# Sixteen weight splits moved from VectorE to GpSimd in a two-FFN, selective-scan layer

## The chip, the cores and the metric

The kernel runs on one core of a Trainium2 chip. The metric is device time in microseconds; lower is better. One core has TensorE (PE in the profile; its weight loads are PEld), VectorE (DVE), ScalarE (ACT), GpSimd (POOL) and SyncE (SP), which here issues the DMAs. Each engine takes its instructions in the order in which they were emitted and waits on semaphores that others raise.

## The reference

Input x is 4 x 1024 x 512 in float32: 4096 rows. The layer is half a feed-forward net, a selective scan, and half a feed-forward net again, each on the normalised rows and each with a residual:

```python
x = x + 0.5 * ffn(layernorm(x))
x = x + attn(layernorm(x))
x = x + 0.5 * ffn(layernorm(x))          # same weights as the first

def ffn(x):                               # gate_w, up_w: 1408 x 512, down_w: 512 x 1408, entries -1, 0, 1
    return ((silu(x @ gate_w.T * gate_s) * (x @ up_w.T * up_s)) @ down_w.T) * down_s

def attn(x):                              # I = 1024 channels, N = 16 states
    h, gate = split(W_in @ x)             # W_in: 2048 x 512
    h = silu(causal_conv4(h) + conv_b)
    ts, B, C = split(Wx @ h)              # 128, 16, 16; each rms-normalised
    delta = softplus(Wdt @ ts + dt_bias)
    # per channel i and state n, over the 1024 time steps of a sequence:
    # s = exp(delta * A[i, n]) * s + delta * B[n] * h ;  y += s * C[n]
    return Wout @ ((y + D * h) * silu(gate))
```

## The kernel before

**Precision.** A matmul in the kernel takes float32 data split in two: a high half that ScalarE makes by copying to TensorE's format, and a low half, the difference between the data and the high half. A product is then the sum of three matmuls (`PARTS`: high by high, high by low, low by high). The weights stand in DRAM as 57 pieces of 128 x 512. All have to be split once. At first use a raw piece is loaded, its high half is written by ScalarE and its low half by the subtraction in question, both into a slot of `wring` (three slots), and the slot is stored to the DRAM buffer `wsp`, from which later uses load it ready-made. The 33 feed-forward pieces are only checked: the reference's weights there are small integers, so that their low halves are zero, and the program takes the branch that leaves them out (`light`). The first three of `W_in`'s pieces and five more are split in the early part from a staging area in `sbuf` (`late` is false: 8 pieces). The other sixteen are the "late" ones, and they alone bear on the change: eight for the gate half of `W_in` (stage `gates`, chunk 0) and eight for `Wout` (stage `post`, chunk 0). Their raw data is loaded into `tb[:, 0..3]` (L1953), ScalarE makes the high half (L1553), VectorE the low half (L1730), and SP stores the slot (L1966).

**Tiling.** The rows are cut in eight chunks (`c`) of 512; two chunks make one sequence. Per chunk there are the stages `ffn1`, `prep_in` (the W_in product, convolution), `dt0` to `dt3` (softplus), `post` (gating and W_out product) and `ffn2`. They form the main stream. Beside it runs the scan stream: per chunk 32 groups (two halves of four 128-channel blocks, 16 states each). For one group GpSimd multiplies delta*h by the row of B (L1890, two instructions of 128 x 1024), ScalarE makes four exponentials (L1517, into two PSUM banks `pa`), VectorE does four scans (L1691), TensorE transposes the result (L1367), and VectorE adds C times it to `acc` (L1702). For three of the sixteen states ScalarE (L1538) and GpSimd (L1903) do this last step. Buffers: `sbuf` three deep, the row of B (`bring`, L2092) two deep. `post` of a chunk comes three chunks behind.

**The rest of GpSimd's work.** It makes the low halves of activations (L1765 in the nets and `post`, L1806 in `prep_in`), residual sums (L1775), and parts of the softplus (L1816 to L1827).

**What sets the order.** `Book` lists the units of every thread (`m` main, `c` convolution, `l` norms, `d` softplus, `s` scan products, exponentials and scans, `t` transposes and sums, `z` setup and weight pieces; the DMAs have one thread each) with the semaphore values that they wait for. `Plan.order` then runs all threads through a model of the engines' durations (`Sketch`) and writes out one fixed order per engine: again and again it takes the unit with the least start time plus 0.01 us times its rank (`FIRST`). On VectorE, `z` has rank 1, before everything but the norms. `FIRST` has no entry for `z` on GpSimd, and a thread without one has rank 9 (`rank.get(name, 9)`), behind the scan's rank 4. Because every choice depends on the model's clock, a changed duration or engine of one unit can change the order of all that follows. In each engine's program a wait holds up everything behind it. In SP's queue the store of a piece (L1966) waits for the low half, and DMAs that stand behind it wait too.

**What waits for a low half.** TensorE's first matmul on the slot (`ring_tok[k] = u.lo`; L1310 in `gates`, L1299 in `post`), the store (L1966), and the next raw load into the same place (`late_tok`).

Of the kernel before, what the change touches and what calls it, by code (L numbers as in the profile page):

```python
# [49 lines left out]
ALU = mybir.AluOpType  # L50
# [203 lines left out]
class Book:  # L254
# [56 lines left out]
    def staged(self, kind, n, slot, k, there, before, late=False):  # L311

        u = self.add("z", Unit(kind))
        u.n, u.slot, u.k, u.there, u.before, u.late = n, slot, k, there, before, late
        u.hi = self.up(self.S.a_piece)
        u.lo = self.up(self.S.v_piece)
        if kind == "checked":
            u.kept = self.pieces[n] = self.up(self.S.st_p[k], 16)
            self.check = u.lo
        else:  # L320
            u.kept = self.pieces[n] = self.up(self.S.st_q[k], 16)
        if not late:
            self.raw_free[k] = (u.lo,)
        self.add("piece_out", u)
        return u
# [778 lines left out]
def macaron(nc, x_in, wp_in, wx_in, wdt_in, const_in, lnw_in, ds_in, ident_in, out):  # L1104
    ctx = ExitStack()
    with ctx:
# [6 lines left out]
        def sem(name):  # L1113
            return ctx.enter_context(nc.semaphore(name))
# [64 lines left out]
        S = Unit("semaphores")  # L1179
# [13 lines left out]
        S.v_g, S.v_tslo, S.v_yu, S.v_yg = sem("v_g"), sem("v_tslo"), sem("v_yu"), sem("v_yg")  # L1193
        S.v_scan, S.v_cmac = sem("v_scan"), sem("v_cmac")

        S.g_const, S.g_one, S.g_ve, S.g_rs, S.g_nb = sem("g_const"), sem("g_one"), sem("g_ve"), sem("g_rs"), sem("g_nb")
        S.g_lo, S.g_sum, S.g_halo, S.g_clo = sem("g_lo"), sem("g_sum"), sem("g_halo"), sem("g_clo")
        S.g_xs, S.g_rr, S.g_bc, S.g_bn, S.g_ct = sem("g_xs"), sem("g_rr"), sem("g_bc"), sem("g_bn"), sem("g_ct")
# [20 lines left out]
        def col(i, n=1):  # L1219
            return cst[:, i:i + n]  # L1220
# [24 lines left out]
        def staged_in(u):  # L1245
            return tb[:, u.k, :] if u.late else sbuf[:, 0, u.k, :]

        def staged_out(u):
            return parts[:, u.slot, :, :].bitcast(F32R) if u.kind == "part" else wring[:, u.slot, :, :]
# [457 lines left out]
        def dve_pieces(units):  # L1707
            def program(q, e):
                for u in units:
                    if u.kind == "consts":  # L1710
                        q.wait_ge(u.there)
                        e.tensor_scalar(csh[:, 0:11], col(C_GS, 11), 0.5, None, ALU.mult).then_inc(S.v_const, 1)
                        yield
                        q.wait_ge(u.gs)
                        e.tensor_tensor(csh[:, 11:22], csh[:, 0:11], col(C_US, 11), ALU.mult)
                        yield
                        e.tensor_scalar(dsb[:, :], dsb[:, :], 0.5, None, ALU.mult)
                        yield
                        e.tensor_scalar(csh[:, 22:66], col(C_DS, 44), 0.5, None, ALU.mult).then_inc(S.v_const, 1)
                        yield  # L1720
                    elif u.kind == "checked":
                        s, half = u.slot
                        q.wait_ge(u.hi)
                        e.scalar_tensor_tensor(staged_in(u), staged_in(u), 1.0, wring[:, s, half, :].bitcast(F32),
                                               ALU.mult, ALU.not_equal,
                                               accum_out=losum[:, u.n:u.n + 1]).then_inc(S.v_piece, 1)
                        yield
                    elif u.kind in ("whole", "part"):
                        q.wait_ge(u.hi)
                        e.tensor_tensor(staged_out(u)[:, 1, :], staged_in(u), staged_out(u)[:, 0, :],  # L1730
                                        ALU.subtract).then_inc(S.v_piece, 1)
                        yield
                    elif u.kind == "flag":
                        q.wait_ge(u.check)
                        e.tensor_reduce(lored[:, 0:1], losum[:, :], mybir.AxisListType.X, ALU.add).then_inc(S.v_flag, 1)
                        yield
                        q.wait_ge(u.sum)
                        e.tensor_scalar(lored[:, 1:2], lored[:, 0:1], 0.0, None, ALU.is_gt).then_inc(S.v_flag, 1)
                        yield
                        q.wait_ge(u.pe)  # L1740
                        e.tensor_copy(flag[:, :], pt[0][0:1, 0:1]).then_inc(S.v_flag, 1)
                        yield
                    elif u.kind == "split_x":
                        q.wait_ge(u.hi)
                        m = slice(u.a * small_m, (u.a + 1) * small_m)
                        e.tensor_tensor(wx_flat[:, 1, m], small_stage[u.a], wx_flat[:, 0, m],
                                        ALU.subtract).then_inc(S.v_small, 1)
                        yield
                    elif u.kind == "split_dt":
                        q.wait_ge(u.there)  # L1750
                        e.tensor_scalar(wd_stage, wd_stage, col(C_TLN), None, ALU.mult).then_inc(S.v_small, 1)
                        yield
                        q.wait_ge(u.hi)
                        e.tensor_tensor(wdts[:, 1, :], wd_stage, wdts[:, 0, :], ALU.subtract).then_inc(S.v_small, 1)
                        yield
            return program
# [150 lines left out]
        def pool_consts(units):  # L1907
            def program(q, e):
                for u in units:
                    if u.kind == "consts":  # L1910
                        e.memset(mone[:, :], -1.0)
                        yield
                        e.memset(mhalf[:, :], -0.5)
                        yield
                        e.memset(bn[:, :, :], 0.0).then_inc(S.g_const, 1)
                        yield
                    elif u.kind == "flag":
                        e.memset(lored[:, 2:3], 1.0).then_inc(S.g_one, 1)
                        yield
            return program  # L1920

# [313 lines left out]
```

## Time and profile before

| | us |
|---|---|
| median of 3 runs | 2909.91 (2907.37 to 2915.78) |
| the profiled execution's own time | 2897.91 |
| its span, first to last instruction | 2896.1 |
| PE / PEld busy | 2419.9 / 1961.3 |
| DVE busy | 2496.7 |
| ACT busy | 1756.8 |
| POOL busy | 2259.9 |

Busy times say how long an engine had an instruction in execution; an instruction that is held up in execution counts as busy. A row of a timeline gives start, duration, engine, line and operation; consecutive instructions of one kind are merged ("x3"), and the bracket gives the idle time before them and what ended it. All times are microseconds from the span's start.

### The profile page before, as it was taken

The numbers are of one execution on the slowest core, as the hardware profiler recorded it, in microseconds if no ns is written. First come the engines' busy times: TensorE is split into PE (matmuls) and PEld (weight loads), VectorE is DVE, ScalarE is ACT, GpSimd is POOL, SyncE is SP. The second block draws the span as 40 slices with busy tenths as digits, with TensorE's granted clock in tenths as the row PEclk, the third lists the DMA queues.
The fourth block names the chain that finished last, engine by engine and source line by source line (L and its number), as shares of the span: only waits on it lengthen the run. The fifth ranks groups of instructions, "written<-read, shape, count | busy, mean of one in ns | idle before, by whom it ended". The sixth has DMA issues, their size and how long they took to land. (4 is left out here: it accounts for less than half of the span.)

```text
span 2896.1 us, 38161 instructions
## 1 busy us (share of the span) xinstructions
PE 2419.9 (84%) x12266; PEld 1961.3 (68%) x12266; DVE 2496.7 (86%) x3131; ACT 1756.8 (61%) x2995; POOL 2259.9 (78%) x1370
## 2 busy tenths in 40 slices
PE   6678879788777998889988899889988896599968
PEld 5466667667665876677766777667766775377757
DVE  5549899799889999899989988798988888999973
ACT  5447568667466665576657665667656667465522
POOL 2237859988976889689997889779896799889852
PEclk9869889899888999899998999889999897599989
DMA  7635573673677467945777366854678378355544
GB/s 269 238 114 167 178 241 107 224 264 121 234 263 260 116 201 254 323 163 186 230 266 285 121 223 226 309 206 149 219 253 289 130 260 307 105 194 189 189 163 142
DMA packets 293951, 606.65 MB, mean 209 GB/s; under 512 B 23024, under 2 KB 23792, under 8 KB 293744
## 3 DMA queue, kind: packets, MB, share of 16 engines
q1 hardware_dynamic: 293744, 604.13, 62.1%
q8 instruction: 101, 1.65, 0.2%
q14 instruction: 106, 0.87, 0.1%
HBM read 451.47 MB, written 152.57 MB: 209 GB/s over the span
## 5 line engine op out<-in xcount | busy, mean ns | idle before, releaser
L1890 POOL TENSOR_TENSOR sbuf<-dus,bring 128x1024 f32<-128x1024 f32 x512 | 1220.9, 2400 | 235.0 <-PE pt L1367 130.3
L1517 ACT ACTIVATE pa<-dls,cst 128x512 f32<-128x512 f32 x1024 | 691.5, 688 | 425.8 <-DVE sbuf L1691 419.2
L1367 PE MATMUL pt<-ident,sbuf 128*128 128x128 f32 x4096 | 660.8, 298 | 230.2 <-DVE sbuf L1691 99.8
L1367 PEld LDWEIGHTS pt<-ident,sbuf 128*128 128x128 f32 x4096 | 513.7, 152 | 392.4 <-DVE sbuf L1691 140.6
L1287 PE MATMUL pm<-xT,wring 128*128 128x512 f32 x2816 | 705.7, 399 | 10.7 <-DVE xT L1574 4.3
L1691 DVE TENSOR_TENSOR_SCAN sbuf<-pa,sbuf 128x512 f32<-128x512 f32 x512 | 608.6, 1211 | 65.6 <-ACT pa L1517 55.7
L1691 DVE TENSOR_TENSOR_SCAN sbuf<-pa,carry,sbuf 128x512 f32<-128x512 f32 x512 | 635.0, 1269 | 25.8 <-ACT pa L1517 19.5
L1702 DVE SCALAR_TENSOR_TENSOR acc<-pt,cT,acc 128x512 f32<-128x512 f32 x768 | 548.5, 739 | 78.4 <-PE pt L1367 74.9
L1299 PE MATMUL pm<-wring,act 128*128 128x512 f32 x2176 | 579.7, 409 | 33.2 <-DMA wring<-wsp 11.2
L1287 PEld LDWEIGHTS pm<-xT,wring 128*128 128x128 f32 x2816 | 516.8, 189 | 113.4 <-issue 14.2
L1310 PE MATMUL pm<-xT,wring 128*128 128x512 f32 x1536 | 427.8, 430 | 74.2 <-DVE hd L1641 29.5
L1299 PEld LDWEIGHTS pm<-wring,act 128*128 128x128 f32 x2176 | 401.4, 193 | 120.7 <-DVE hd L1619 16.0
L1310 PEld LDWEIGHTS pm<-xT,wring 128*128 128x128 f32 x1536 | 308.1, 208 | 148.0 <-issue 56.3
L1765 POOL TENSOR_TENSOR act<-hd,act 128x512 fp32r<-128x512 f32 x240 | 310.2, 1298 | 116.6 <-ACT act L1400 115.7
L1903 POOL TENSOR_TENSOR acc<-acc,tmp 128x512 f32<-128x512 f32 x192 | 248.1, 1292 | 45.5 <-ACT tmp L1538 45.1
L1400 ACT ACTIVATE act<-hd 128x512 fp32r<-128x512 f32 x240 | 149.1, 623 | 89.1 <-DVE hd L1619 71.7
L1538 ACT ACTIVATE tmp<-pt,cT 128x512 f32<-128x512 f32 x192 | 130.9, 682 | 89.2 <-POOL acc L1903 76.4
L1396 ACT ACTIVATE th<-pm,csh 128x512 f32<-128x512 f32 x176 | 119.9, 681 | 84.6 <-PE pm L1287 84.0
L1579 DVE SCALAR_TENSOR_TENSOR aa<-th,pm 128x512 f32<-128x512 f32 x176 | 118.1, 671 | 50.4 <-ACT th L1396 50.0
L1323 PE MATMUL pm<-wxs,act 128*128 128x160 f32 x768 | 131.8, 332 | 19.4 <-DVE hd L1641 19.4
L1583 DVE SCALAR_TENSOR_TENSOR hd<-aa,csh,pm 128x512 f32<-128x512 f32 x176 | 129.8, 738 | 17.1 <-PE pm L1287 12.5
L1806 POOL TENSOR_TENSOR act<-hd,act 128x512 fp32r<-128x512 f32 x64 | 82.1, 1283 | 74.9 <-ACT act L1458 69.8
(129 smaller groups left out, 2286.1 us busy)
## 6 DMA issues: line engine op xcount, KB each, us to landing
wring<-wsp SPq DMA_DIRECT2D x408, 512.0 KB, 4.6
bring<-b_d SPq DMA_DIRECT2D x256, 256.0 KB, 4.0
xn_d<-tb SPq DMA_DIRECT2D x24, 1024.0 KB, 9.6
xnb<-xn_d SPq DMA_DIRECT2D x19, 1024.0 KB, 7.4
x_d<-tb SPq DMA_DIRECT2D x16, 1024.0 KB, 6.0
u_d<-hd SPq DMA_DIRECT2D x64, 256.0 KB, 4.5
sg_d<-hd SPq DMA_DIRECT2D x64, 256.0 KB, 4.0
tb<-x_d SPq DMA_DIRECT2D x16, 1024.0 KB, 7.0
```

What stands on the lines that cost most here:

```text
L1287: ins = e.matmul(pm[b][:, :], wring[:, slot, up if light else pw, k * P:(k + 1) * P], xT[:, px, k, :], start=(pw, px, k) == (0, 0, 0), sto ...
L1299: ins = e.matmul(pm[u.bank[tt]][:, :], act[:, px, u.k, tt * P:(tt + 1) * P], wring[:, u.slot, pw + u.half, :], start=u.first and (pw, px) ...
L1310: ins = e.matmul(pm[u.bank][:, :], wring[:, u.slot, pw, k * P:(k + 1) * P], xT[:, px, k, :], start=(pw, px, k) == (0, 0, 0), stop=end)
L1323: ins = e.matmul(pm[u.bank[tt // 2]][:, (tt % 2) * XW:(tt % 2 + 1) * XW], act[:, pw, u.k, tt * P:(tt + 1) * P], wxs[:, px, u.k, :], start= ...
L1367: ins = e.matmul(pt[u.pt[tt]][:, k * P:(k + 1) * P], sbuf[:, u.s3, k, tt * P:(tt + 1) * P], ident[:, :], is_transpose=True, start=True, st ...
L1400: e.activation(act[:, 0, u.k, :], hd[:, u.h, :], ACT.Copy).then_inc(S.a_hi, 1)
L1517: e.activation(pa[k % 2][:, :], dls[:, k, :], ACT.Exp, scale=col(C_A + (4 * u.ig + k) * N + u.n)).then_inc(S.a_exp, 1)
L1691: e.tensor_tensor_scan(d, pa[k % 2][:, :], d, init, ALU.mult, ALU.add).then_inc(S.v_scan, 1)
L1702: e.scalar_tensor_tensor(acc[:, tt, :], pt[u.pt[tt]][:, :], cT[:, u.c % 4, tt, u.n:u.n + 1], acc[:, tt, :], ALU.mult, ALU.add).then_inc(S. ...
L1765: e.tensor_tensor(act[:, 1, u.k, :], hd[:, u.h, :], act[:, 0, u.k, :], ALU.subtract).then_inc(S.g_lo, 1)
L1890: e.tensor_tensor(sbuf[:, u.s3, h * m:(h + 1) * m, :], dus[:, h * m:(h + 1) * m, :], bring[:, u.s2:u.s2 + 1, :].broadcast_to([P, m, TC]), ...
L1903: e.tensor_tensor(acc[:, tt, :], acc[:, tt, :], tmp[:, :], ALU.add).then_inc(S.g_cadd, 1)
```

## The change

The low half of a late piece is now made by a GpSimd unit in thread `z`, with a semaphore of its own. All who waited for the old one wait for the new one. The operation, its operands and the number of instructions are the same. Units that are not late stay on VectorE. Nothing is added to `FIRST`.

```diff
@@ staged
-        u.lo = self.up(self.S.v_piece)
+        u.lo = self.up(self.S.g_piece if late else self.S.v_piece)
@@ macaron
+        S.g_piece = sem("g_piece")
@@ dve_pieces
-                    elif u.kind in ("whole", "part"):
+                    elif u.kind in ("whole", "part") and not u.late:
                         q.wait_ge(u.hi)
                         e.tensor_tensor(staged_out(u)[:, 1, :], staged_in(u), staged_out(u)[:, 0, :],
                                         ALU.subtract).then_inc(S.v_piece, 1)
@@ pool_consts
+                    elif u.kind == "whole" and u.late:
+                        q.wait_ge(u.hi)
+                        e.tensor_tensor(staged_out(u)[:, 1, :], staged_in(u), staged_out(u)[:, 0, :],
+                                        ALU.subtract).then_inc(S.g_piece, 1)
+                        yield
```

## Rows read from the trace of the kernel before

**Rows 1.** The page's busy times (share of the span) and instruction counts
```profile
PE 2419.9 (84%) x12266; PEld 1961.3 (68%) x12266; DVE 2496.7 (86%) x3131; ACT 1756.8 (61%) x2995; POOL 2259.9 (78%) x1370
```
**Rows 2.** Busy time by stretch: start:end, length, engines, granted clock, DMA share, GB/s
```profile
200.00:2797.00 2597.00, 2209.56 (x11370) 1786.93 (x11371) 2361.10 (x2883) 1641.78 (x2792) 2188.78 (x1292) 0.91 0.63 212
```
**Rows 3.** The same view of L1730 alone: DVE busy and count by stretch
```profile
130.00:180.00 50.00, 2.05 (x3) 0.62 0.49 178
180.00:215.00 35.00, 11.27 (x5) 0.81 0.34 120
755.00:800.00 45.00, 9.10 (x2) 0.81 0.53 186
800.00:835.00 35.00, 10.29 (x6) 0.90 0.80 280
```
**Rows 4.** The timeline of VectorE
```profile
138.11 0.68 DVE L1730 TENSOR_TENSOR wring<-tb,wring 128x512 fp32r<-128x512 f32 x1
...
198.94 8.38 DVE L1730 TENSOR_TENSOR wring<-tb,wring 128x512 fp32r<-128x512 f32 x3
207.25 1.21 DVE L1691 TENSOR_TENSOR_SCAN sbuf<-pa,sbuf 128x512 f32<-128x512 f32 x1
...
210.31 2.19 DVE L1730 TENSOR_TENSOR wring<-tb,wring 128x512 fp32r<-128x512 f32 x1
...
755.41 0.75 DVE L1702 SCALAR_TENSOR_TENSOR acc<-pt,cT,acc 128x512 f32<-128x512 f32 x1 [8.14 <-PE pt L1367]
...
763.31 7.53 DVE L1730 TENSOR_TENSOR wring<-tb,wring 128x512 fp32r<-128x512 f32 x1
...
777.03 1.57 DVE L1730 TENSOR_TENSOR wring<-tb,wring 128x512 fp32r<-128x512 f32 x1
```
**Rows 5.** The timeline of GpSimd
```profile
198.07 3.15 POOL L1890 TENSOR_TENSOR sbuf<-dus,bring 128x1024 f32<-128x1024 f32 x1
...
204.07 7.89 POOL L1890 TENSOR_TENSOR sbuf<-dus,bring 128x1024 f32<-128x1024 f32 x3
220.09 13.96 POOL L1890 TENSOR_TENSOR sbuf<-dus,bring 128x1024 f32<-128x1024 f32 x6 [8.13 <-DMA bring<-b_d]
...
760.89 9.41 POOL L1890 TENSOR_TENSOR sbuf<-dus,bring 128x1024 f32<-128x1024 f32 x4
775.66 5.15 POOL L1890 TENSOR_TENSOR sbuf<-dus,bring 128x1024 f32<-128x1024 f32 x2 [5.36 <-DMA bring<-b_d]
```
**Rows 6.** The timeline of SP's DMA issues
```profile
212.53 0.32 SPq L1966 DMA_DIRECT2D wsp<-wring  x1
...
213.44 0.76 SPq L2092 DMA_DIRECT2D bring<-b_d  x1
...
770.87 0.32 SPq L1966 DMA_DIRECT2D wsp<-wring  x1
771.24 1.26 SPq L2092 DMA_DIRECT2D bring<-b_d  x2
```
**Rows 7.** The timeline of TensorE
```profile
201.82 10.88 PE L1310 MATMUL pm<-xT,wring 128*128 128x512 f32 x36 [7.88 <-DVE wring L1730]
...
812.04 2.50 PE L1299 MATMUL pm<-wring,act 128*128 128x512 f32 x5 [3.00 <-DVE wring L1730]
```
**Rows 8.** The page's groups of GpSimd: count, busy, mean ns of one, idle before
```profile
L1890 POOL TENSOR_TENSOR sbuf<-dus,bring 128x1024 f32<-128x1024 f32 x512 | 1220.9, 2400 | 235.0 <-PE pt L1367 130.3
...
L1765 POOL TENSOR_TENSOR act<-hd,act 128x512 fp32r<-128x512 f32 x240 | 310.2, 1298 | 116.6 <-ACT act L1400 115.7
```
**Rows 9.** Groups of GpSimd between 807 and 835
```profile
L1890 POOL TENSOR_TENSOR sbuf<-dus,bring 128x1024 f32<-128x1024 f32 x5 | 13.7, 2743 | 0.0
```
**Rows 10.** Busy time by stretch, columns as in rows 2
```profile
740.00:760.00 20.00, 17.36 (x85) 12.79 (x84) 11.53 (x13) 9.60 (x15) 20.00 (x12) 1.00 0.94 340
760.00:780.00 20.00, 12.22 (x55) 9.60 (x54) 20.00 (x15) 4.90 (x8) 14.64 (x7) 0.83 0.24 70
...
810.00:835.00 25.00, 20.32 (x93) 16.25 (x94) 24.35 (x23) 13.67 (x20) 25.00 (x12) 0.86 0.80 280
```

## The prediction, made before the changed kernel had run

> **What bounds the kernel now.** I read the page's busy times first: VectorE leads with 86% of the span, TensorE has 84%, GpSimd 78% [rows 1]. An average over the whole span hides the start and the tail, so next I asked for the stretch in which scans run, 200 to 2797 us: VectorE is busy 2361.1 of 2597 us, 90.9%, GpSimd 2188.8, 84.3%, TensorE 2209.6, 85.1% [rows 2]. So VectorE is the nearest to a bound, but no engine is full: VectorE's last 9% are short waits in a loop of exponential, scan, transpose and sum. A microsecond taken from VectorE is worth at most one, and one added to GpSimd costs between nothing and one.
>
> Third, the moved instruction by itself. The sixteen late splits stand in four stretches with 2.05, 11.27, 9.10 and 10.29 us, 32.7 us together [rows 3]. That is much more than their work: with GpSimd idle one takes 0.68 us [rows 4], so sixteen would take 10.9. The other 21.8 us are contention, and the timelines show with whom. The split at 763.31 took 7.53 us, to 770.84 [rows 4]; GpSimd ran four products back to back from 760.89 to 770.30, and VectorE's instruction ended half a microsecond after the last [rows 5]. The three at 198.94 took 8.38 us beside GpSimd's products [rows 4, 5].
>
> The Trainium skill (SBUF — State Buffer, "Who interferes with whom") states that a VectorE instruction with two SBUF inputs and a GpSimd instruction that reads SBUF share one port pair, which is an exclusive lock: whoever is first holds it for its whole instruction. The trace agrees that the split is held up, but the rule's "until the first finishes" would let the split in after at most one product, 2.40 + 0.68 = 3.1 us, and the row has 7.53. By the rule alone the excess of 16 pieces would be at most 16 x 2.4 = 38 us, which bounds it no better than the 21.8 that the rows give.
>
> Fourth, who stands behind such a stall. TensorE waited 7.88 us for the first slot in `gates` and 3.00 in `post` [rows 7]. SP had the store of the slot ahead of the next loads of B's row: the store went at 770.87, the loads at 771.24, right after the split ended, and GpSimd, out of rows, idled 5.36 us until 775.66; the same at 212.53 and 213.44 with 8.13 us idle [rows 5, 6]. The plan books far less for the split than it took, so the store stands too early in SP's order. Granted clock was 1.00 at 740 to 760 and 0.83 in the 20 us of the second stall [rows 10], which slows TensorE's work after it; I give that no term of its own.
>
> **The change part by part.** The sum is made against the profiled execution's 2897.91 us.
>
> Removed from VectorE: 32.7 us [rows 3]. Added to GpSimd: 16 x 1.298 = 20.8 us, by the row of the same operation and shape, which reads SBUF twice and writes the same type [rows 8]. It cannot hold itself up. The number of DMAs, their sizes and the ScalarE copies stay.
>
> (a) Three pieces in `prep_in` (0.68 us each, [rows 3, 4]). The main stream is not near their use: cost and gain 0. If the cover were gone it would be 3 x (1.30 - 0.68) = 1.9 us.
>
> (b) Five pieces in `gates`. The first scan starts at 207.25, behind the three held-up splits [rows 4]; its product was ready at 198.07 + 3.15 = 201.22 [rows 5]. So the scan stream can start 6.0 us sooner. Against it: on GpSimd the pieces have rank 9, the products rank 4, so the planner puts them behind the four products that the two rows of B allow. They then come near 209 us and not at 201.8, and the main stream on TensorE stands some 7 us longer. GpSimd's 8.13 us of idle time [rows 5] holds four of the five (4 x 1.30 = 5.2). One stream gains 6, the other loses as much: between 0 and 6.0, and I take 3.
>
> (c) Two pieces at 763 and 777: VectorE loses 9.10 us to them [rows 3]. It is back to back behind each, so the upper end is 9.1. The lower end comes from GpSimd: it was full from 740 to 760 [rows 10], and just before, VectorE had idled 8.14 us waiting for a sum that GpSimd's part held up [rows 4]; if GpSimd is what paces here, the gain is only its idle 5.36 less the two new instructions, 2.6, so 2.8. Halfway is 6.
>
> (d) Six pieces at 811 to 829: VectorE loses 10.29 us [rows 3]. GpSimd is full for all 25 us from 810 to 835 [rows 10] and gets 6 x 1.30 = 7.8 us more. It gets back what the splits cost it: five products took 2743 ns there and not 2400 [rows 8, 9], 1.7 us, and with the other instructions in that stretch, in proportion to its 25 us (25/13.7), some 3.1. Net +4.7 for GpSimd, -10.3 for VectorE. If the two take turns as the bound, 10.3 - 4.7 = 5.6; the ends are -4.7 (GpSimd alone paces) and 10.3. I take 5.
>
> (e) The new wait. GpSimd's instruction waits for ScalarE's high half, made just before. Behind it in GpSimd's program stand products, and behind those the scans. The planner's `Sketch` books 0.16 + 512/474 = 1.24 us for this instruction on GpSimd, and the row has 1.298 [rows 8]; on VectorE it booked 0.05 + 512/962 = 0.58, and the sixteen took 2.04 on average (32.7 / 16). So the wait should now be planned in the right place, as today's was not. 0, and with each of 13 pieces 0.3 us late, 4.
>
> (f) SP. Stores now stand where the plan expects a GpSimd piece to end; the two jams of rows 6 go. This is contained in (b) and (c).
>
> (g) All orders after 138 us are written anew, since the planner's clock moves. Nothing in the rows says in which direction; I carry +-8 us for it, the size of the largest single waits above (8.38 and 8.14) [rows 4].
>
> Sum: 3 + 6 + 5 = 14 us less. 2897.9 - 14 = 2883.9. The median of the runs shown is 2909.9, 12.0 us above the profiled execution; with the same offset the forecast is 2896 us. My own range for this case: the low ends 0 + 2.8 - 4.7 and the high ends 6.0 + 9.1 + 10.3 give -2 to 25 us of gain, so 2885 to 2912; I give it 2885 to 2905 as its core.
>
> **The rivals.**
>
> *VectorE was the whole bound (chance 0.12).* For it: 90.9% busy, and every held-up split is followed by work at once [rows 2, 4]. Then all 32.7 us come back: 2877. Against it: GpSimd is full in two of the three stretches [rows 10], and at 755 VectorE idled 8.14 us.
>
> *Given back later (0.22).* What the scan stream gains is lost at the next place where it waits for the main stream or for GpSimd: b gives nothing, c gives 2.8, d gives 0, and (e) eats it: 2907 to 2910. For it: VectorE idles 9% of the scanning stretch even now [rows 2], so each stream already waits for the other engines at times. Against it: the stalls come while VectorE or GpSimd is full [rows 10], where there is little slack to swallow a gain.
>
> *GpSimd becomes the bound, because its pieces go last (0.18).* Ten pieces are made while GpSimd is busy (four in b, six in d; [rows 4, 10]). With rank 9 each can come behind one product: 2.40 + 1.30 = 3.7 us, 37.0 us in all, as a delay of TensorE's slot. Today TensorE waits 7.88 + 3.00 = 10.9 us for these [rows 7]. So the main stream loses 26.1 us while VectorE gains 14: +12, 2922. It decides from the point where TensorE's waits for the slot exceed some 25 us. For it: GpSimd is full in 740 to 760 and 810 to 835. Against it: three slots. A piece of `Wout` is used for 12 matmuls (four row blocks, three products), and two others stand between its making and its use, so one product's delay should be hidden. The Trainium skill (GPSIMD Engine Reference, "Engine selection") speaks for this rival: elementwise work belongs on VectorE, GpSimd being about twice slower; the rows agree on the ratio, 1.298 to 0.68 us, but leave the stall out of it.
>
> *The change does not do what it says:* all sixteen late units are of the kind "whole", so none is lost between the two new conditions; 0.
>
> **How the numbers follow.** The forecast's case has 0.48, VectorE whole 0.12, given back 0.22, GpSimd bound 0.18. A difference under about 0.3%, 8.7 us, cannot be told from none, so faster is below 2901.2 and slower above 2918.6. Faster: 0.42 of the first, 0.12, 0.02 of the third, together 0.56. Slower: 0.13 of the last, 0.01 of the third, 0.14. The same: 0.30. The range for 8 in 10: 2876, the whole bound, to 2920, short of the last rival's full price.
>
> **What would show it.** L1730 should be left with 8 instructions, and a GpSimd line should have 16 of `wring<-tb,wring` near 1.3 us (right if 1.25 to 1.4; wrong if they too are held up to 3 us). GpSimd's busy time should rise by 16 to 21 us, and VectorE's fall by 30 to 33. The first scan should start near 201 us (b). SP should have no load of B's row behind a late store for more than 2 us, and the two idles of 8.13 and 5.36 us should shrink. TensorE's waits for `wring` from GpSimd should stay under 15 us in total; over 25 the slower rival has it. If VectorE's busy time falls by 30 and the span by less than 5, the gain was given back, and the place is where the two traces' scans, counted from the start, come level again. I am wrong if VectorE's stalls were already covered by GpSimd's pace.

## The result, and the profile after

The changed kernel takes 2936.86 us (median of 4 runs, 2929.07 to 2941.40) against 2908.64 for the kernel before in the same rounds: ratio 1.0089, 95% interval 1.0064 to 1.0115. It is slower. The forecast was 2896 (2876 to 2920), faster; the time is outside the range and on the other side. The profiled execution took 2929.07 us. Ratios here and below leave out the few executions that ran far slower than the rest, two of the twelve of `g_rank35` (3163 and 10567 us) among them.

The page of the changed kernel, span and busy times:

```profile
span 2927.2 us, 38155 instructions
...
PE 2437.4 (83%) x12266; PEld 1977.5 (68%) x12266; DVE 2472.9 (84%) x3115; ACT 1756.2 (60%) x2995; POOL 2278.2 (78%) x1386
```

Beside [rows 1]: VectorE lost 16 instructions and 23.8 us, GpSimd gained 16 and 18.3 us, and yet the span grew by 31.1 us. The move was made and its sizes were nearly those forecast. Of the busy times, the splits' own instructions make up 33.0 and 21.5 us; the rest lies with the other instructions and was not followed. So the time went into waiting. The timeline of GpSimd in `post` of chunk 0 shows where (L1923 is the split, L1891 the product, L1904 the sum, L1817 to L1828 softplus):

```profile
778.98 2.48 POOL L1923 TENSOR_TENSOR wring<-tb,wring 128x512 fp32r<-128x512 f32 x2
...
810.00 2.38 POOL L1891 TENSOR_TENSOR sbuf<-dus,bring 128x1024 f32<-128x1024 f32 x1
812.31 2.38 POOL L1817 TENSOR_TENSOR spw<-spw,spe 128x1024 f32<-128x1024 f32 x1
814.62 4.70 POOL L1891 TENSOR_TENSOR sbuf<-dus,bring 128x1024 f32<-128x1024 f32 x2
...
842.60 2.39 POOL L1891 TENSOR_TENSOR sbuf<-dus,bring 128x1024 f32<-128x1024 f32 x1
844.92 2.55 POOL L1923 TENSOR_TENSOR wring<-tb,wring 128x512 fp32r<-128x512 f32 x2
```

ScalarE's high half of that split:

```profile
812.84 0.63 ACT L1554 ACTIVATE wring<-tb 128x512 fp32r<-128x512 f32 x1 [0.36 <-DMA tb<-wp_in]
```

The high half was ready at 813.47 (812.84 + 0.63) and the split was taken up at 844.92, 31.4 us later. GpSimd had no idle time in between: 16 products, sums and softplus steps, the first of them begun at 812.31, ran before it. TensorE's main matmuls of `Wout` (L1300) by stretch (columns as in rows 2, with PE and PEld alone), then the whole core over the gap:

```profile
740.00:820.00 80.00, 31.81 (x112) 21.48 (x112) 0.86 0.67 234
820.00:845.00 25.00, 0.00 (x0) 0.00 (x0) 0.50 0.38 130
```

```profile
810.00:845.00 35.00, 16.83 (x73) 12.25 (x72) 30.47 (x32) 21.52 (x31) 35.00 (x19) 0.57 0.48 160
```

The main stream stood from 810.45 to 846.27, and TensorE's granted clock fell to 0.50 of full speed, its lower level of 1.2 GHz, while it made only transposes. The view of waits does not show this as one long wait for the slot (TensorE waited for it 5.2 us at most): the planner had put transposes of the scans into the gap. A planned gap shows in no list of waits. It shows when the same instruction is timed in both traces.

The same had happened before, in `gates`. Three of its splits, ready at 198.2, 198.7 and 208.5, were taken up 25.0, 30.4 and 21.8 us later, behind eight products and more:

```profile
223.13 1.27 POOL L1923 TENSOR_TENSOR wring<-tb,wring 128x512 fp32r<-128x512 f32 x1
...
229.03 2.52 POOL L1923 TENSOR_TENSOR wring<-tb,wring 128x512 fp32r<-128x512 f32 x2
```

There the main stream made it good: it was 11 us late at 343 and 1 us at 569. How long a split is held does not say by itself what it costs (`g_gates_only` below tests it).

Lateness against the kernel before of the n-th instruction of a kind (us, positive is later), from the two traces (one execution of each kernel, 31.1 us apart in span where the medians are 28.2 apart):

| at (before) | 241 | 569 | 676 | 845 | 1020 | 1182 | 1348 | 1687 | 2019 | 2297 |
|---|---|---|---|---|---|---|---|---|---|---|
| main stream (low half of xT) | +4.7 | +1.1 | +5.6 | +39.1 | +36.4 | +31.5 | +38.0 | +29.9 | +27.7 | +31.1 |

| at (before) | 245 | 380 | 694 | 834 | 933 | 1218 | 1287 | 1399 | 1575 | 2034 | 2695 |
|---|---|---|---|---|---|---|---|---|---|---|---|
| scans | -7.5 | -22.0 | +0.6 | -14.0 | -40.0 | -56.2 | +14.7 | +21.5 | +27.4 | +27.7 | +31.5 |

The scans ran ahead on what the main stream lost, by 56 us at 1218. Then they met their input. Their products need `dus`, which comes out of the main stream's softplus by way of DRAM. In the changed kernel at the start of chunk 3's scans, from the timelines of VectorE and SP (L2074 stores it, L2090 loads it):

```profile
1164.06 1.27 DVE L1692 TENSOR_TENSOR_SCAN sbuf<-pa,carry,sbuf 128x512 f32<-128x512 f32 x1
...
1203.00 0.43 SPq L2074 DMA_DIRECT2D du_d<-spw  x1
...
1209.85 0.91 SPq L2090 DMA_DIRECT2D dus<-du_d  x2
...
1218.94 2.46 DVE L1692 TENSOR_TENSOR_SCAN sbuf<-pa,carry,sbuf 128x512 f32<-128x512 f32 x2 [3.61 <-POOL sbuf L1891]
```

No scan ran from 1165.33 to 1218.94, and the scans went from 55.5 us ahead to 1.8 ahead in one step. (The list of waits shows little of this too. It puts 3.61 us down to the products, and VectorE's longest idle time in there, 20.01 us before 1207.42, to TensorE's L1300.) The second half of chunk 3 brought the rest, from 9 us late to 27:

```profile
1392.62 9.41 POOL L1891 TENSOR_TENSOR sbuf<-dus,bring 128x1024 f32<-128x1024 f32 x4 [5.98 <-DMA dus<-du_d]
```

From 1575 on both streams are some 24 to 32 us late, to the end.

### The profile page after: what moved, and what is told of

Same layout as the page of the kernel before. It is cut to its first block and busy times, and to the rows that moved or that the text cites. A ratio compares the mean times of both kernels' runs of the same rounds, so it can differ in the third digit from the quotient of the medians.

```text
span 2927.2 us, 38155 instructions
## 1 busy us (share of the span) xinstructions
PE 2437.4 (83%) x12266; PEld 1977.5 (68%) x12266; DVE 2472.9 (84%) x3115; ACT 1756.2 (60%) x2995; POOL 2278.2 (78%) x1386
## 5 line engine op out<-in xcount | busy, mean ns | idle before, releaser
L1891 POOL TENSOR_TENSOR sbuf<-dus,bring 128x1024 f32<-128x1024 f32 x512 | 1216.0, 2391 | 210.4 <-PE pt L1368 96.7
L1368 PE MATMUL pt<-ident,sbuf 128*128 128x128 f32 x4096 | 667.9, 301 | 254.5 <-DVE sbuf L1692 119.5
L1368 PEld LDWEIGHTS pt<-ident,sbuf 128*128 128x128 f32 x4096 | 523.6, 154 | 414.3 <-DVE sbuf L1692 165.0
L1300 PE MATMUL pm<-wring,act 128*128 128x512 f32 x2176 | 578.3, 409 | 30.6 <-DMA wring<-wsp 11.3
L1300 PEld LDWEIGHTS pm<-wring,act 128*128 128x128 f32 x2176 | 401.4, 192 | 119.1 <-DMA wring<-wsp 15.9
L1766 POOL TENSOR_TENSOR act<-hd,act 128x512 fp32r<-128x512 f32 x240 | 311.7, 1303 | 130.0 <-ACT act L1401 129.0
L1904 POOL TENSOR_TENSOR acc<-acc,tmp 128x512 f32<-128x512 f32 x192 | 248.4, 1294 | 57.7 <-ACT tmp L1539 57.7
L1324 PEld LDWEIGHTS pm<-wxs,act 128*128 128x128 f32 x768 | 120.6, 243 | 13.7 <-issue 7.0
```

The costliest lines, as they stand in the source:

```text
L1300: ins = e.matmul(pm[u.bank[tt]][:, :], act[:, px, u.k, tt * P:(tt + 1) * P], wring[:, u.slot, pw + u.half, :], start=u.first and (pw, px) ...
L1324: ins = e.matmul(pm[u.bank[tt // 2]][:, (tt % 2) * XW:(tt % 2 + 1) * XW], act[:, pw, u.k, tt * P:(tt + 1) * P], wxs[:, px, u.k, :], start= ...
L1368: ins = e.matmul(pt[u.pt[tt]][:, k * P:(k + 1) * P], sbuf[:, u.s3, k, tt * P:(tt + 1) * P], ident[:, :], is_transpose=True, start=True, st ...
L1766: e.tensor_tensor(act[:, 1, u.k, :], hd[:, u.h, :], act[:, 0, u.k, :], ALU.subtract).then_inc(S.g_lo, 1)
L1891: e.tensor_tensor(sbuf[:, u.s3, h * m:(h + 1) * m, :], dus[:, h * m:(h + 1) * m, :], bring[:, u.s2:u.s2 + 1, :].broadcast_to([P, m, TC]), ...
L1904: e.tensor_tensor(acc[:, tt, :], acc[:, tt, :], tmp[:, :], ALU.add).then_inc(S.g_cadd, 1)
```

## The experiments

Each is timed against the kernel before in the same rounds. "On GpSimd" and "rank" are those of the late splits.

| label | kernel | median us | ratio (95%) |
|---|---|---|---|
| changed | GpSimd, rank 9 | 2936.86 | 1.0089 (1.0064-1.0115) |
| g_rank1 | GpSimd, rank 1 | 2921.73 | 1.0032 (1.0018-1.0046) |
| g_rank35 | GpSimd, rank 3.5 | 2899.85 | 0.9952 (0.9934-0.9970) |
| g_post_only | eight of `post` on GpSimd, rank 9 | 2953.99 | 1.0133 (1.0104-1.0163) |
| g_gates_only | eight of `gates` on GpSimd, rank 9 | 2909.33 | 0.9988 (0.9970-1.0005) |
| v_rank9 | VectorE, rank 9 | 2965.32 | 1.0185 (1.0156-1.0213) |
| v_margin | VectorE, MARGIN 0.32 | 2930.56 | 1.0073 (1.0047-1.0099) |
| v_margin2 | VectorE, MARGIN 0.27 | 2920.94 | 1.0034 (1.0017-1.0051) |
| g9_m32 | GpSimd, rank 9, MARGIN 0.32 | 2947.68 | 1.0118 (1.0089-1.0148) |
| g9_m27 | GpSimd, rank 9, MARGIN 0.27 | 2947.42 | 1.0128 (1.0101-1.0154) |
| g35_m32 | GpSimd, rank 3.5, MARGIN 0.32 | 2912.16 | 1.0006 (0.9991-1.0021) |
| g35_m27 | GpSimd, rank 3.5, MARGIN 0.27 | 2899.03 | 0.9959 (0.9944-0.9975) |
| v_narrow | VectorE, 8 columns, order of before | 2903.85 | 0.9982 (0.9968-0.9996) |
| v_memset | VectorE, zeros, order of before | 2890.51 | 0.9917 (0.9891-0.9943) |
| g_in_place | GpSimd, order of before | 2904.44 | 0.9980 (0.9963-0.9997) |
| g_held | the same, third split 10 us later | 2909.93 | 0.9991 (0.9973-1.0009) |
| v_early | `Wout` split before `dt0`, VectorE | 2912.80 | 1.0009 (0.9990-1.0027) |

**g_rank1**

```diff
-    "pool": dict(l=0, m=1, c=1, d=2, t=3, s=4),
+    "pool": dict(l=0, z=1, m=1, c=1, d=2, t=3, s=4),
```

> All sixteen late splits on GpSimd as in the changed kernel, but thread z has rank 1 there (it had none, so 9). Theory (starvation by rank): in the changed kernel three pieces of post 0 had their high halves at 813 to 815 us and GpSimd took the first up at 844.92, after 31 us of products, sums and softplus; TensorE's main stream stood from 810.5 to 846.3. With rank 1 that gap must go (TensorE's waits for wring from GpSimd under 5 us), the main stream at post 0 must be no later than in the kernel before, and the time comes to 2885 to 2905 us, that is 30 to 50 below the changed kernel. Rival (GpSimd is simply too slow or too full for them: 20.8 us more work): the time stays within 8 us of the changed kernel's 2937. Rival (any new order of the planner costs some 1%): it also stays well above 2909.

The gap went: the main stream was 23 us ahead of the kernel before at 845 where it had been 39 late. But the time only came down to 2922, 15 of the 28 us, against the 2885 to 2905 expected. Now the scans were late, by 43 us at 834, and the end was paced by them: the main stream was still 7 us ahead at 2297, the scans 42 late at 2417, and both 23 late from 2581. One new wait of VectorE stands right behind splits of `Wout` (GpSimd made three at 794.53 and one each at 802.20, 805.79 and 809.74, with softplus steps between, and only then the sum):

```profile
DVE acc L1703 <- POOL acc L1904: 7.5, 1, 7.5
```

So splits in front of everything on a full GpSimd hold back work for which VectorE waits. That is only part of it. The scans were 28 us late at 712 already, before the first split of `Wout` (756.31), and the version with rank 3.5 below was 25 late there; rank 1 added 15 us by 834, rank 3.5 added 6. What made the first 25 to 28 us was not tried. Nor does this run exclude that an order other than the old one costs its 9 us, whatever the rank; the three margins below bear on that.

**g_post_only, g_gates_only**

```diff
-        u.lo = self.up(self.S.g_piece if late else self.S.v_piece)
+        u.lo = self.up(self.S.g_piece if late and n >= WO else self.S.v_piece)    # gates_only: n < WO
...                                 # the same condition where VectorE and GpSimd emit the split
```

> Only the eight pieces of Wout (stage post) go to GpSimd, rank 9; the eight of gates stay on VectorE. If the gap in post 0 is the cause, this has the same gap of about 30 us in TensorE's main stream and costs 20 to 35 us over the kernel before. If the loss came from the start of the scans (gates), it is within 9 us of before.

> Only the eight pieces of gates go to GpSimd, rank 9; the eight of Wout stay on VectorE. In the changed kernel the main stream was 5 to 12 us late after gates but level again at 568 us, so the theory expects within 9 us of before, 2900 to 2918; the rival (gates, or a new order as such, is the cause) expects over 2925.

Both as the theory had it for the place: the move in `gates` costs nothing, the move in `post` costs it all and more (1.0133, 42 us by the medians, over the 20 to 35 expected). Why it loses more than the changed kernel, 42 us against 28, is open. Its third split began at 852.15, and L1300 paused from 819.8 to 853.46. In `g_gates_only` the splits of `gates` were held just as in the changed kernel (24.9, 30.3 and 21.8 us), and the time did not suffer.

**v_rank9**

```diff
-    "dve": dict(l=0, z=1, m=1, c=1, d=2, t=3, s=4),
+    "dve": dict(l=0, m=1, c=1, d=2, t=3, s=4),
```

> The kernel before with all splits on VectorE, but thread z without a rank there too (9 in place of 1). Theory (the rank starves the pieces on a full engine, whichever it is): the splits in post 0 now come behind VectorE's scans and sums, the main stream stands there, and the time is 10 to 35 us over before. It also holds back the first splits (checked pieces), in which VectorE competes with nothing of a better rank than 1 but the norms and the net's own products, at most 5 us. Rival (rank does not matter, the engine does): within 9 us of before.

The worst of all, 1.0185, above the expected range, with no split on GpSimd. VectorE took up the first two splits of `Wout` 17.2 and 40.8 us after their high halves were ready (0.0 and 0.3 in the kernel before), L1299 paused from 777.14 to 836.84, and the main stream was 49 us late at 845. A rank behind everything starves a split on either of the two engines.

**v_margin, v_margin2: what a new order alone is worth**. `MARGIN` is the time in us that the planner adds, for most threads, before it counts another engine's result as ready. To change it changes the order and nothing else.

```diff
-MARGIN = 0.3
+MARGIN = 0.32        # v_margin2: 0.27
```

> The kernel before with the planner's MARGIN at 0.32 in place of 0.30: the same instructions on the same engines in another order. It measures what a new order alone is worth. Theory (the loss of the changed kernel is the starved splits, not the new order): within 10 us of before. Rival (any new order costs): 15 us or more over before, as the kernel before would then be a lucky order.

> The same with MARGIN at 0.27, a second sample: within 10 us of before by the theory, over 15 above by the rival. Together they give the size of a difference that needs no other cause.

1.0073 and 1.0034, 19 and 9.5 us by the medians: the first lies outside what the theory allowed and inside the rival's range, the second just inside what the theory allowed. The kernel before has a favourable order, and another can start 0.3 to 0.7% behind, though not every one does (`g_gates_only`, 0.9988). So the runs so far leave open how much of the changed kernel's 0.9% is its order. Hence the next four.

Both traces have one wait that the kernel before does not have. Near 2375 VectorE waited 21.6 and 22.9 us for the products, while GpSimd waited 19.2 and 19.4 us for the load of `dus`. The same wait, 20.9 to 22.3 us, stands in `g_post_only`, `v_rank9`, `v_early`, `g35_m32` and both kernels with rank 9 of the next group, and not in the changed kernel or `g_rank35`. The main stream was already 17 and 12 us late at 2297 in the two, so the wait shows where the scans met it and not what delayed it; that stays open.

**g9_m32, g35_m32, g9_m27, g35_m27**: the changed kernel, and the one with `z=3.5` on GpSimd (below), at the two other margins.

> The changed kernel (rank 9) with the planner's MARGIN at 0.32, where the kernel before came to 1.0073. Theory (starved splits cost, whatever the rest): the trace shows splits of Wout held over 15 us behind other GpSimd work, the main stream 20 us or more late by 850 us, and the time is 2930 to 2960. Rival (a bad draw): it is under 2925, or as slow without any gap.

> Rank 3.5 with MARGIN 0.32: 2900 to 2930 by the theory, at least 10 us under the same margin with rank 9. If rank 3.5 at 0.30 was luck, this is as slow as rank 9.

> The changed kernel (rank 9) with MARGIN at 0.27, where the kernel before came to 1.0034: by the theory 2925 to 2955, with the same gap in TensorE's main stream at post 0; by the rival under 2925.

> Rank 3.5 with MARGIN 0.27: 2895 to 2925 by the theory, at least 10 us under rank 9 at the same margin. It also says whether the gain of rank 3.5 over the kernel before (0.9952) holds over a second and third order or was one draw.

Ratios to the kernel before at three margins:

| MARGIN | VectorE, rank 1 | GpSimd, rank 9 | GpSimd, rank 3.5 |
|---|---|---|---|
| 0.27 | 1.0034 | 1.0128 | 0.9959 |
| 0.30 | 1 | 1.0089 | 0.9952 |
| 0.32 | 1.0073 | 1.0118 | 1.0006 |

All four came out in their expected ranges. Along each line the order is the same: rank 9 is 0.5 to 0.9% over VectorE, rank 3.5 is 0.5 to 0.8% under it. Three lines that agree make a mere draw of the order unlikely. The sizes are rough, since another margin changes the rest of the order too and each column differs by 0.4 to 0.7% within itself. About half of the gap is made good later: at equal margin the main stream with rank 9 is 39 to 47 us behind that of VectorE at 845, and 17 to 28 us are left in the medians. The gap is there in all with rank 9; GpSimd's split that was held, at MARGIN 0.32 and 0.27, and TensorE's first main matmul behind it at 0.32:

```profile
844.96 2.53 POOL L1923 TENSOR_TENSOR wring<-tb,wring 128x512 fp32r<-128x512 f32 x2
```

```profile
843.73 2.50 POOL L1923 TENSOR_TENSOR wring<-tb,wring 128x512 fp32r<-128x512 f32 x2
```

```profile
846.30 1.98 PE L1300 MATMUL pm<-wring,act 128*128 128x512 f32 x4
```

The main stream was 38.7 and 40.0 us late at 845.

**g_rank35**

```diff
-    "pool": dict(l=0, m=1, c=1, d=2, t=3, s=4),
+    "pool": dict(l=0, m=1, c=1, d=2, t=3, s=4, z=3.5),
```

> The changed kernel with rank 3.5 for thread z on GpSimd: ahead of the products alone, behind sums, softplus and activations. Rank 9 starved the main stream (+36 us at post 0), rank 1 kept it 22 us ahead but left the scans 43 us behind at 834 us. If a balance is to be found between, it is here: 2900 to 2920, scans and main stream both within 15 us of before at 850 us. If any order that differs costs 10 to 20 us, as the two orders with another margin did (1.0073 and 1.0034), it is 2918 to 2935.

0.9952, at the lower edge of the first range: faster than both kernels, by 11.3 us under the kernel before and 37 under the changed one. Its splits of `Wout` were taken up 0.1 to 3.6 us after their high halves were ready, and the main stream was 26 us ahead at 845. The scans were still 31 us late at 834, not within 15 as expected, but caught up by 2034 (+0.3). This is the version to keep, though at margin 0.32 it is no faster than the kernel before (1.0006). Its page:

```profile
span 2893.6 us, 38162 instructions
...
PE 2423.6 (84%) x12266; PEld 1968.5 (68%) x12266; DVE 2468.1 (85%) x3115; ACT 1757.4 (61%) x2995; POOL 2277.7 (79%) x1386
```

**v_narrow and v_memset: the stall by itself, in the exact order of the kernel before**

```diff
+                        w = 8 if u.late and not isinstance(e, Sketch) else 512
+                        e.tensor_tensor(staged_out(u)[:, 1, 0:w], staged_in(u)[:, 0:w], staged_out(u)[:, 0, 0:w],
...
                         # v_memset, for late units, in place of this:
+                            e.memset(staged_out(u)[:, 1, :].bitcast(F32), 0.0).then_inc(S.v_piece, 1)
```

> The kernel before, in its exact order on every engine, but each late split is emitted 8 columns wide and not 512; the low halves of the gate and Wout weights are left incomplete. It takes most of the 32.7 us of the sixteen from VectorE, adds nothing to GpSimd and moves nothing. Theory (VectorE's held-up splits were covered: where GpSimd is full, VectorE's freed time turns into waiting): the time falls by less than 12 us, VectorE's idle time rises by over 15. Rival (they were on the path, as the forecast had it): it falls by 20 to 33 us. If a narrow split is still held until GpSimd's next gap, its 7.5 us stays, and the trace shows it.

> The kernel before in its exact order, but each late low half is filled with zeros by VectorE (a memset, which reads nothing) and not computed; the gate and Wout products lose that part. In the narrow run a split of 8 columns was still held for up to 7.0 us, so most of the stall stayed; a write without SBUF inputs should not be held (0.2 to 0.7 us each), and VectorE is rid of about 25 to 30 us. Theory (covered: other engines pace there): the time falls by 3 to 15 us, less than half of what VectorE is rid of. Rival (the forecast: VectorE's stalls are on the path): 20 us or more.

VectorE's row for the split of [rows 4] that took 7.53 us, in the narrow run and as a memset:

```profile
763.54 7.00 DVE L1731 TENSOR_TENSOR wring<-tb,wring 128x8 fp32r<-128x8 f32 x1
```

```profile
764.64 0.48 DVE L1731 MEMSET wring<- 128x512 f32 x1
```

With a sixty-fourth of the columns (the other 504 of each low half are left unwritten) it was still held 7 us, so that run freed VectorE of 11.8 us only (2496.7 to 2484.9) and gained 0.18%. The time fell by less than 12 us, as the theory had it, but VectorE's idle time rose by 8.6 us and not by the 15 that it also asked for; this run alone decides little.

The memset reads nothing, is never held (all sixteen 485 ns), frees 22.8 us, and gained 0.83%, 17 to 32 us (20.7 by the medians). That is the rival's value, not the theory's: what held VectorE was on the path in good part. It was not VectorE's time alone. The first split's store went at 765.15 and not at 770.87 (770.57 in the narrow run), so it no longer held up the loads of B's row behind it. GpSimd, which idles 5.36 us before 775.66 in the kernel before ([rows 5]) and 4.86 there in the narrow run, ran six products without a pause from 762.12. There are two reserves. The trace does not show the gain: the run was 10.4 us ahead at 845, behind its last edit, and 5 us late at the end; but that execution (2905.30) was the slowest of the six, the others taking 2883.90 to 2893.48. And the run leaves zeros as the low halves that all later chunks multiply by. How much of the 24 us comes from that data was not tried.

**g_in_place and g_held: the move alone**

```diff
+        moved = [w for w in when["dve"] if w[1] is not None]          # (planned time, piece)
+        out["dve"] = [n for n, w in zip(out["dve"], when["dve"]) if w[1] is None]
+        names, times = out["pool"], [w[0] for w in when["pool"]]
+        for at, piece in moved:
+            at += 0.0                    # g_held: 10.0 for the third piece of Wout
+            i = max(last, next((i for i, t in enumerate(times) if t >= at), len(times)))
+            names.insert(i, "z")
...                                # and GpSimd emits the split where the planner had VectorE
```

> All sixteen late splits on GpSimd, but the planner plans them on VectorE: every other instruction of every engine keeps the order of the kernel before, and each split stands in GpSimd's program at the planned time that it had on VectorE. This is the move alone, without starvation and without a new order. Theory: within 9 us of before, rather under it (2900 to 2915), since VectorE loses stalls that were mostly covered and GpSimd gains 20.8 us where it is full; the loss of the changed kernel is all in the order that the planner made of it. Rival (GpSimd's extra work is the price): 15 us or more over before.

> The same as the kernel in place, but the third split of Wout (and so those behind it) stands 10 us later in GpSimd's program; nothing else differs (31 us as in the changed kernel would make the engines wait for each other in a circle in this order). Theory (a held slot stops TensorE's main stream, and what it loses comes back at the end nearly in full): 6 to 12 us over the kernel in place. Rival (such a delay is swallowed by the two other slots or by slack later): within 3 us of it.

In place the move is worth 0.2%, some 6 us: less than the memset's 24 or so. The rest is what GpSimd's added work can have cost, which is an argument by difference and carries the memset's reserve with it. Held back by 10 us, TensorE's wait for the slot was

```profile
826.39 2.50 PE L1313 MATMUL pm<-wring,act 128*128 128x512 f32 x5 [15.40 <-POOL wring L1938]
```

where it was 5.9 in place, but the time rose by 3 to 5.5 us (ratios, medians), below the expected 6 to 12. The two profiled executions differ by 15, nothing of it made good, but that of `g_held` was the slowest of its twelve. I count this one as inconclusive on the share that is given back.

**v_early**

```diff
+            if c == 0 and self.light:
+                self.split_all(list(range(WO, WO + 8)))
             self.dt0(c)
...                                # and `post` of chunk 0 loads them ready-made
```

> All splits on VectorE, but the eight pieces of Wout are split before dt0 of chunk 0, from sbuf to sbuf and stored to wsp, where VectorE once idled 24 us and GpSimd 20; post 0 then loads them ready-made. No split stands beside a full GpSimd in post 0. If the held-up splits in post 0 (19.4 us of VectorE) were on the path: 8 to 20 us under before. If they were covered: within 8 us of before, 2904 to 2920. A cost of up to 4 us can come at the start, when the raw loads and stores meet the last pieces of W_in.

1.0009. No split stood in `post`, the main stream was 16 us ahead at 845, and the end was 17 us late in the trace. It has a new order too, and two such orders cost 10 and 19 us. The run cannot tell a gain taken back by the order from no gain, so I draw nothing from it.

## Why the prediction was wrong

**The step that failed is (e), the new wait**, and with it the size of the last rival. I wrote that "the wait should now be planned in the right place" and priced it at 0 to 4 us; the rival let each split come "behind one product: 2.40 + 1.30 = 3.7 us". I knew the rank of 9 and took it for a lost tie, once: against the products' 4 it is a handicap of 0.05 us of the planner's clock. In (b) I even let the rank put pieces behind four products, and then priced (e) without it. But on an engine that is full every choice is a tie: each instruction that becomes ready meanwhile has the same earliest start and a better rank. [Rows 10] had shown GpSimd busy 25.00 of 25 us in just this stretch. The split waited for 16 instructions, 31.4 us, and TensorE's main stream stood for 35.8 us. That the rank did it is shown on both engines: with it on VectorE the same stream stops (`v_rank9`), and with 3.5 in its place on GpSimd the holds in `post` shrink to 3.6 us at most, and the time is 1.1 to 1.7% lower at each of three margins. A plan with right durations places such a wait exactly, and exactly too late.

Point by point:

- *Removed and added work.* VectorE 32.7 us less, GpSimd 20.8 more: measured 23.8 and 18.3 as busy time, outside the 30 to 33 and inside the 16 to 21 that I had named. The splits alone come to 33.0 and 21.5, as forecast; the rest is in other instructions. The splits on GpSimd took 1283 ns at the median (1298 forecast), one of them 2247.
- *(a)* Nothing at `prep_in`: g_gates_only, 0.9988, fits.
- *(b)* 3 us from the earlier first scan. It began at 207.1 and not at 201, since the first products (204.62) came after one split and both softplus steps; but the scans were 7.5 us ahead at 245. The later pieces did not come near 209, behind four products, but at 223.13 to 230.3, behind eight and more. `g_gates_only` puts the whole between 9 us gained and 1 lost. The 3 us lie in that interval, as nothing does; the mechanism was wrong.
- *(c), (d)* 11 us from `post`. With the starvation taken away the move is worth 0.5 to 0.8% at equal margin, 14 to 22 us, and rank 3.5 at margin 0.30 gives 2900 where the forecast was 2896. That nearness proves no term of the sum: in the old order (`g_in_place`) the whole move is worth 6 to 7 us of the 14, and no run measures (c) or (d) alone.
- *(f)* The jams of SP went from these two places: GpSimd's waits for B's row were 34.4 us in the kernel before and 25.1 in the changed one. Its waits for `dus` rose from 26.4 to 42.0 instead.
- *(g)* A new order at no cost, +-8 us. Two samples of it cost 10 and 19 us. It should have been a term with a sign: an order that is replaced is rarely replaced by an equal one when the old one is good.
- *The rival "GpSimd becomes the bound"* was the right one in kind, since its pieces did go last, with the wrong price, +12 for +28, and a condition that did not hold as I wrote it ("from the point where TensorE's waits for the slot exceed some 25 us"). Its counter-argument, the three slots, failed because three splits in a row were held: all three slots of the ring stood empty of low halves at once. TensorE's matmuls waited 8.3 us for such a slot in `gates` and 5.2 in `post`, 13.5 together, under the 15 that should have cleared the forecast, since the gap of 35.8 us was planned full of transposes. I had looked for the loss in a list that cannot show it.
- *The rule of the Trainium skill on the lock* (SBUF — State Buffer, "Who interferes with whom"): the narrow run shows that the holding time does not depend on the split's own size (7.00 us with 8 columns, 7.53 with 512), and the memset that an instruction without SBUF inputs is not held (485 ns), as the page says. Nine splits of the narrow run were held over 0.5 us. Eight of them ended within 0.05 us of the end of the GpSimd instruction that ran when they began, which is the rule to the letter. The ninth, the one of 7.00 us, let two such ends pass, at 765.90 and 768.22, and ended 0.02 us after the third, behind which GpSimd had run out of work. No run explains that one.

## What to carry to other kernels

When an operation moves to another engine under a list scheduler, look up its priority there first: on a full engine the lowest rank is not a lost tie but a wait until the engine runs empty, or until what outranks it is done (here 31.4 us), and the stream behind it can stop for as long. What that costs depends on the place: equal holds in `gates` cost nothing. Try at least two or three planner settings on both sides before you credit or blame the move, as two new orders alone cost 0.3 and 0.7% here. And compare the n-th instruction of each stream between traces: a gap that the plan has filled with other work is in no list of waits.

## What the runs showed of the hardware that was not expected

A VectorE subtraction with both inputs in SBUF beside back-to-back GpSimd products was mostly held only until the running GpSimd instruction ended. But at times it was held until GpSimd ran out of work: 7.53 us in the kernel before, 7.0 us in its place with only 8 columns to do, 7.53 us in `v_margin`, and 7.13 and 10.08 us in `v_margin2`. The last was the first of these three, and four more GpSimd instructions ran back to back after the one that it met, the last ending at 811.04:

```profile
801.51 11.28 DVE L1730 TENSOR_TENSOR wring<-tb,wring 128x512 fp32r<-128x512 f32 x3
```

A memset of 512 columns in the place of the first one took 0.48 us.
